# Letting the adding scatters of one expert's blocks be in flight together in a routed feed-forward kernel

## What is computed

```python
x = x + jnp.tanh(g_xattn[0]) * _L0_xattn_ref(_layernorm(x), ctx_512, ...)
x = x + jnp.tanh(g_ffn[0])   * _L0_ffn_ref(_layernorm(x), ...)     # 8 experts, top 2, hidden 192
x = x + jnp.tanh(g_xattn[1]) * _L1_xattn_ref(_layernorm(x), ctx_512, ctx_512, ...)
x = x + jnp.tanh(g_ffn[1])   * _L1_ffn_ref(_layernorm(x), ...)     # 16 experts, top 6, hidden 352
```

```python
weights = jnp.take_along_axis(probs, idx, axis=1)            # idx: the TOP_K experts of a token
cw = jnp.einsum('tk,tke->te', weights, onehot)
h = silu(xf @ W1.T + B1) * (xf @ W3.T + B3)                  # for every expert
y = y + c[:, None] * (h @ W2.T + B2)
```

## Time and profile before

| | |
|---|---|
| median of 3 runs | 2453.0 us (2446.0 to 2457.29) |
| the profiled execution's own time | 2450.1 us |
| its span, first to last instruction | 2448.2 us |
| mean granted TensorE clock | 0.898 of full speed |
| PE busy | 1968.5 us (80%) |
| DVE / ACT / POOL busy | 1245.5 / 815.7 / 1015.5 us |
| HBM traffic | 147 GB/s over the span |
| queue q0 (POOL's DMAs) | 33600 packets, 79.73 MB |

### The profile page before, as it was taken

One profiled execution on the slowest core, in us unless ns is written; L12 is line 12 of the kernel. 1 busy time (PEld: TensorE's weight loads), 2 busy tenths in 40 slices (PEclk: granted clock), 3 DMA queues, 4 the chain that ended last, 5 costly groups with the idle time before them and its releaser, 6 DMA issues. The chain is left out here.

```text
span 2448.2 us, 36252 instructions
## 1 busy us (share of the span) xinstructions
PE 1968.5 (80%) x10825; PEld 1599.1 (65%) x10825; DVE 1245.5 (51%) x2625; ACT 815.7 (33%) x1315; POOL 1015.5 (41%) x795
## 2 busy tenths in 40 slices
PE   4559989886782655878776887899999879999995
PEld 2247767765561443555444676779999778989995
DVE  7864553322221866788875566544444323434442
ACT  3451111132331454565674311113333222323331
POOL 5443644633343566675772110014342333433331
PEclk7779989998895677988988998999999889999998
DMA  8565846977756465221454000094649788474444
GB/s 296 167 241 181 257 126 227 288 229 224 178 116 145 120 152 159 40 36 34 110 149 153 21 29 26 1 338 85 156 80 286 227 280 239 84 224 80 80 80 107
DMA packets 130433, 370.56 MB, mean 151 GB/s; under 512 B 20456, under 2 KB 24424, under 8 KB 125080
## 3 DMA queue, kind: packets, MB, share of 16 engines
q1 hardware_dynamic: 83320, 264.33, 34.2%
q0 software_dynamic: 33600, 79.73, 17.5%
q10 hardware_dynamic: 13344, 24.32, 2.7%
HBM read 209.93 MB, written 149.74 MB: 147 GB/s over the span
## 5 line engine op out<-in xcount | busy, mean ns | idle before, releaser
L1582 PE MATMUL ps<-f_wb,f_xThi 128*128 x2088 | 541.7, 341 | 34.3 <-issue 24.6
L1698 POOL DMA_INDIRECT y_scratch<-f_yo,f_rows x150 | 238.2, 1588 | 495.1 <-ACT f_yo L1426 270.0
L1582 PEld LDWEIGHTS ps<-f_wb,f_xThi 128*128 128x128 f32 x2088 | 375.2, 194 | 63.1 <-issue 53.8
L1582 PE MATMUL ps<-f_wb,f_xTlo 128*128 x1044 | 348.7, 334 | 0.0
L1601 PE MATMUL ps<-f_wb,f_hThi 128*128 (+2 forms) x822 | 281.0, 423 | 16.1 <-DVE f_hTlo L1909 15.6
L728 POOL TENSOR_TENSOR a_elo<-a_e,a_ehi 128x768 f16<-128x768 f32 x128 | 217.4, 1704 | 159.4 <-ACT a_ehi L785 158.0
L1677 POOL DMA_INDIRECT f_xg<-xn_scratch,f_rows x150 | 159.2, 1061 | 217.8 <-PE ps L1566 161.5
L1927 DVE TENSOR_TENSOR f_g<-ps,f_bb 128x352 f32<-128x352 f32 x111 | 58.2, 524 | 342.2 <-PE ps L1582 263.7
L1426 ACT ACTIVATE f_yo<-ps,f_share 128x512 f32<-128x512 f32 x150 | 103.3, 689 | 299.1 <-PE ps L1601 186.4
L1582 PEld LDWEIGHTS ps<-f_wb,f_xTlo 128*128 128x128 f32 x1044 | 202.1, 194 | 0.0
L962 DVE TENSOR_REDUCE a_nmax<-ps 128x1 f32<-128x512 f32 x256 | 163.8, 679 | 48.7 <-PE ps L817 48.3
(11 more groups left out here) (241 smaller groups left out, 3897.6 us busy)
## 6 DMA issues: line engine op xcount, KB each, us to landing
f_wb<-w_scratch SPq DMA_DIRECT2D x16, 2816.0 KB
w_scratch<-f_stage_up SPq DMA_DIRECT2D x27, 1024.0 KB, 5.3
w_scratch<-a_stage_up SPq DMA_DIRECT2D x25, 1024.0 KB, 5.3
f_stage_raw<-in_f_w_dram SPq DMA_DIRECT2D x29, 768.0 KB, 7.4
f_wb<-w_scratch SPq DMA_DIRECT2D x16, 1024.0 KB
w_scratch<-f_stage_down SPq DMA_DIRECT2D x108, 128.0 KB
w_scratch<-a_stage_down SPq DMA_DIRECT2D x100, 128.0 KB, 2.3
f_wb<-w_scratch SPq DMA_DIRECT2D x8, 1536.0 KB
```

The costliest lines, as they stand in the source:

```text
L1582: mm = pe.matmul(out, xt[:, b % 2, k, :], weights(at, w, k, low), start=(m == 0), stop=(m == 3 * KD - 1))
L1698: pool.indirect_dma_start(y_d, bass.IndirectOffsetOnAxis(ap=rows_of[:, b:b + 1], axis=0), yo[:, b % 3, :], None, bounds_check=ROWS + P - 1 ...
```

## The change

Scatters of blocks that belong to the same expert touch different rows (a token is at most once in an expert), so they need not wait for each other. The change counts scatters in three semaphores, `scattered[b % 3]`. A scatter now waits for those of b-1 and b-2, each to a count read from two new rows of `table`: the full count where block b is the first of another expert than b-1, and one scatter less (which has landed anyway) where b and b-1 have the same expert. These counts are made by DVE in `tables`. Only the first blocks of layer 0 have fixed, full counts. The spare rows are tripled, one set for each `b % 3`, so that blocks in flight together don't share a spare row either. ACT's and SP's waits keep their meaning.

```diff
+SPARE = 3 * P
...
-        xn_d = [nc.dram_tensor(f"xn{i}_scratch", (ROWS + P, D + m["E"]), F32, kind="Internal").ap()
+        xn_d = [nc.dram_tensor(f"xn{i}_scratch", (ROWS + SPARE, D + m["E"]), F32, kind="Internal").ap()
...
-        scattered = ctx.enter_context(nc.semaphore("scattered"))
+        scattered = [ctx.enter_context(nc.semaphore(f"scattered{i}")) for i in range(3)]
...
-                    sp.dma_start(g["xn_d"][i][ROWS:ROWS + P, :], zero[:, 0:D + m["E"]]).then_inc(zero_out, 16)
-                    sp.dma_start(g["y_d"][i][ROWS:ROWS + P, :], zero[:, 0:D]).then_inc(zero_out, 16)
+                    for to, width in ((g["xn_d"][i], D + m["E"]), (g["y_d"][i], D)):
+                        sp.dma_start(to[ROWS:ROWS + SPARE, :].rearrange("(r p) d -> p r d", p=P),
+                                     zero[:, 0:width].rearrange("p (o d) -> p o d", o=1).to_broadcast([P, 3, width])
+                                     ).then_inc(zero_out, 16)
...
+        def sums_of(b):
+
+            return 16 * ((EARLIER + 2 - b % 3) // 3 + b // 3 + 1)
+
         def added(eng, b):
 
-            if b > 0:
-                eng.wait_ge(scattered, 16 * (EARLIER + b))
+            if b >= 0:
+                eng.wait_ge(scattered[b % 3], sums_of(b))
...
-                added(sp, BLOCKS)
+                for b in range(BLOCKS - 3, BLOCKS):
+                    added(sp, b)
...
-                    added(act, b - 2)
+                    added(act, b - 3)
...
                     pool.wait_ge(yo_ready, b + 1)
-                    added(pool, b)
+                    past = range(max(b - 2, 0), b)
+                    need = [sums_of(other) if EARLIER + other < 3 else
+                            pool.value_load(table[0:1, 1 + b - other, b:b + 1], min_val=16, max_val=sums_of(other))
+                            for other in past]
+                    for other, value in zip(past, need):
+                        pool.wait_ge(scattered[other % 3], value)
+                        pool.sem_inc(earlier_added, 1)
                     pool.indirect_dma_start(y_d, bass.IndirectOffsetOnAxis(ap=rows_of[:, b:b + 1], axis=0),
-                                            yo[:, b % 3, :], None, bounds_check=ROWS + P - 1,
-                                            compute_op=ALU.add).then_inc(scattered, 16)
+                                            yo[:, b % 3, :], None, bounds_check=ROWS + SPARE - 1,
+                                            compute_op=ALU.add).then_inc(scattered[b % 3], 16)
...
+                    link(dve.tensor_tensor(alike[0:1, 1:BLOCKS], ebf[0:1, 1:BLOCKS], ebf[0:1, 0:BLOCKS - 1],
+                                           ALU.is_equal))
+                    for back in range(1, 3):
+                        for r in range(3):
+                            last = dve.scalar_tensor_tensor(
+                                out=wants[0:1, back - 1, back + r:BLOCKS:3],
+                                in0=iota[0:1, 0:len(range(back + r, BLOCKS, 3))],
+                                scalar=float((EARLIER + 2 - r) // 3 + 1), in1=alike[0:1, back + r:BLOCKS:3],
+                                op0=ALU.add, op1=ALU.subtract)
+                    link(last)
+                    for back in range(1, 3):
+                        dve.tensor_scalar(table[0:1, 1 + back, back:BLOCKS], wants[0:1, back - 1, back:BLOCKS], 16.0,
+                                          None, ALU.mult)
...
-                    link(dve.tensor_scalar(red[:, 0:1], lane[:, 0:1], float(PAD_ROW + 1), None, ALU.add))
-                    link(dve.tensor_scalar(padv[:], at, 0.0, red[:, 0:1], ALU.is_equal, ALU.mult))
+                    for r in range(3):
+                        dve.tensor_scalar(red[:, r:r + 1], lane[:, 0:1], float(PAD_ROW + P * r + 1), None, ALU.add)
+                    link(dve.tensor_copy(padv[:, 0:1], lane[:, 0:1]))
+                    for r in range(3):
+                        last = dve.tensor_scalar(padv[:, r:BLOCKS:3], ps[:, XB, r:BLOCKS:3], 0.0, red[:, r:r + 1],
+                                                 ALU.is_equal, ALU.mult)
+                    link(last)
```

More of the change, by code:

```diff
@@ L80, in build @@
         ps = ctx.enter_context(nc.psum_tensor("ps", [P, 8, 512], F32))
-        xn_d = [nc.dram_tensor(f"xn{i}_scratch", (ROWS + P, D + m["E"]), F32, kind="Internal").ap()
+        xn_d = [nc.dram_tensor(f"xn{i}_scratch", (ROWS + SPARE, D + m["E"]), F32, kind="Internal").ap()
                 for i, m in enumerate(MOE)]
-        y_d = [nc.dram_tensor(f"y{i}_scratch", (ROWS + P, D), F32, kind="Internal").ap() for i in range(2)]
+        y_d = [nc.dram_tensor(f"y{i}_scratch", (ROWS + SPARE, D), F32, kind="Internal").ap() for i in range(2)]
         bias_d = nc.dram_tensor("bias_scratch", (MOE[1]["E"], 2, MOE[1]["H"]), F32, kind="Internal").ap()
@@ L1091, in mixture @@
         share = sb(ctx, tag + "share", [P, BLOCKS])
-        table = sb(ctx, tag + "table", [1, 3, BLOCKS], I32)
+        table = sb(ctx, tag + "table", [1, 5 if BIASED else 4, BLOCKS], I32)
         first_of = sb(ctx, tag + "first_of", [1, E + 1], I32)
@@ L1135, in mixture @@
                 padv = sb(route, tag + "padv", [P, BLOCKS])
+                alike = sb(route, tag + "alike", [1, BLOCKS])
+                wants = sb(route, tag + "wants", [1, 2, BLOCKS])
             room = sb(early, tag + "room", [P, SIZE])
@@ L1191, in mixture @@
         out_done = sem("out_done")
+        earlier_added = sem("earlier_added")
         PARAMS = 16 * (3 if BIASED else 2)
@@ L1678, in gather @@
                                             bass.IndirectOffsetOnAxis(ap=rows_of[:, b:b + 1], axis=0),
-                                            bounds_check=ROWS + P - 1).then_inc(gathered[b % 3], 16)
+                                            bounds_check=ROWS + SPARE - 1).then_inc(gathered[b % 3], 16)
                 pool.wait_ge(up_mm, LAST_U)
@@ L1815, in tables @@
                     e, third, at, need, third_of = (
-                        tnum[0:1, 0, :], tnum[0:1, 1, :], table[0:1, 0, :], table[0:1, 1, :], table[0:1, 2, :])
+                        tnum[0:1, 0, :], tnum[0:1, 1, :], table[0:1, 0, :], table[0:1, 1, :],
+                        table[0:1, 4, :] if BIASED else tnum[0:1, 1, :])
                     link(dve.tensor_copy(e, ebf[0:1, :]))
@@ L1923, in _ @@
                     if BIASED:
-                        buf = dve.value_load(table[0:1, 2, b:b + 1], min_val=0, max_val=2)
+                        buf = dve.value_load(table[0:1, 4, b:b + 1], min_val=0, max_val=2)
                         dve.wait_ge(g_mm, b + 1)
```

## The result

| | before | changed |
|---|---|---|
| median of the runs | 2455.1 us (4 runs, 2446.0 to 2457.3) | 2415.7 us (4 runs, 2406.7 to 2418.2) |
| ratio, 95% interval | 1 | 0.984 (0.9804 to 0.9876) |
| profiled execution | 2450.1, span 2448.2 | 2406.7, span 2404.9 |
| the same kernel once more, beside other runs | 2451.9 | 2408.0, ratio 0.9835 (0.9793 to 0.9877), span of its profile 2393.3 |

The forecast was 2402 us (2384 to 2440). The change took 39 us off, 44 in the second measurement, where 50 to 53 were forecast: faster, as said, by some 80 to 90% of the amount.

A forecast was written before the change was run, and what follows sets the result against it. Layer 0 was taken as bound by the serial scatter chain and fetch-delayed landings, layer 1 by PE. -30 - 9 - 12 - 1.5 + 3 = -49.5 us from 2450.1 gave 2400.6; with the median 2.9 above, forecast 2402 us (2384 to 2440).

The forecast's parts named there:

- The bound: Layer 0: serial scatter chain at 5.70 us a block, 5 us more per weight fetch; layer 1: PE at 6.77.
- POOL's own round is ... 4.7 us (bounds 3.7 and 5.9): POOL's time per block, two table loads at 1.0 us included; under PE's 5.52 and 6.77, so hidden.
- Of the 39.6 us I take three quarters, 30 us: Layer 0, blocks 7 to 38: PE's 39.6 us over its own pace, of which 30 us were to be gained.
- End of layer 0, -9: Last scaling to reload of x: last scatter lands at 757.3 against 766.50 us, 9 us gained (bounds 5 and 10).
- Layer 1, -12: Small experts with back-to-back fetches: 12 of 15.4 us lost over six blocks gained; nothing where PE runs at 6.77.
- End of layer 1, -1.5: After the last scaling: last scatter could start at 2426.3 instead of 2428.34 us; 1.5 us gain taken.
- DVE, +3: Nine small instructions more in `tables`, three in `rows`: 1.0 and 0.5 us, in both layers 3 us, not hidden.
- everything else at nothing: POOL's loads taken as hidden behind PE's pace; zeroing three spare-row sets at the start costs nothing, up to 14 us uncovered.
- The sum: Whole kernel: -30 - 9 - 12 - 1.5 + 3 = -49.5 us; forecast 2402 us, chance 0.68.
- The first rival: Gathers queue behind scatters on POOL's one queue, PE still waits for rows: -23.5 us, about 2428; chance 0.17.
- The second: Long waits all lie at expert changes, only both layers' ends gain: -6 us, about 2447; chance 0.10.
- The third: Dear register loads make POOL's round the bound, 7.0 us at 1.65 each: +29 us, about 2479; chance 0.05.

The follow-up runs named there:

- the runs with one layer alone: Changed kernel with the overlap in layer 0 alone: 2426.8 us, 0.9909 of the kernel before; in layer 1 alone: 2445.9 us, 0.9964.
- the cheap table and POOL's loads first: Changed kernel with constant table parts written earlier, fewer DVE operations on PE's path, and POOL's loads ahead of its wait: 2400.4 us, 0.9791 of the kernel before.
- again: Second profile of the changed kernel, nothing altered, from its repeat beside other runs: 2408.0 us, 0.9835 of the kernel before.

## Why the prediction was right, and where it wasn't

- **The bound.** Right. Layer 0 was set by the chain of scatters at 5.70 us a block and by its slow landings beside fetches. Two experiments bear it out: a faster PE alone changes nothing, and the overlap with all else equal is worth 34 us there.
- **"POOL's own round is ... 4.7 us (bounds 3.7 and 5.9)".** Too long. It is 3.26: I added the loads to a round in which they are hidden, and added 0.75 us for the next start where 0.30 is enough once the scatter has nothing to wait for. The lower bound that the text gave for the loads, nothing, was the right end, for a POOL that is behind. Beside it, the Trainium skill, page "DMA: Bandwidth & Descriptors", section on latency and other measured facts, has a floor of about 0.6 us for a register load. The measured median on POOL is 0.289 us; the measurement decides, and the page's price would have been too high.
- **"Of the 39.6 us I take three quarters, 30 us".** About right. Over the six profiles with this loop the blocks of layer 0 gained 21.5, 32.1, 28.9, 28.3, 26.8 and 23.5 us, 27 in the mean.
- **End of layer 0, -9.** -8.3 and -8.8, right. With POOL's loads ahead of the wait it is -10.1, -10.1 and -10.2.
- **Layer 1, -12.** Too small: -17.9. I let the small experts keep a fifth of their loss because they "still drain at each change". They do (11.7 us at one scatter), but POOL catches up 3.5 us with each block, not the 2.1 that a round of 4.7 gives, so that nothing reaches PE. This is the same error in POOL's round, seen from the other side; with the round lengthened to 5.06 the gain went.
- **End of layer 1, -1.5.** Wrong, +0.4 and +0.8. The last scatter starts 4.57 us after the scaling, as before (4.52). Before, the result was there at 2424.51 us and the landing that POOL waited for at 2426.28, 1.8 us later. In the changed kernel this wait is gone, but the two loads with their register work and the waits behind them take the same 1.8 us there (2380.78 to 2382.60, one load of them 0.86). With the loads ahead of the wait the 1.3 us come. And the forecast took 0.75 us from the counts to the start, where the last scatter of layer 1 needs 2.06 in the kernel before, in the changed one (2382.60 to 2384.66) and with the loads first; what these 2.06 us are isn't known.
- **DVE, +3, and everything else at nothing.** This is the step that failed. The additions cost 12 us (7 to 18). DVE's own part was nearly right: PE's waits for its sums, at tables and rows of layer 0 and of layer 1, grew from 2.50, 0.76, 2.13 and 0.97 us before to 3.85, 1.20, 3.49 and 1.42 in the run with full counts, 3.6 us together. What was put at nothing without a reason is what longer waits do to PE's clock, 1.3 to 1.8 us in layer 1 wherever it stayed at half speed for 6.8 us, and the loads where nothing hides them, 1.5 us over the two ends with full counts. These come to 6.4 to 6.9 us, the low end of what was measured. The rest is not placed.
- **The sum.** That the gains came out at 52 us for 52.5 is in part luck. By the runs with one layer alone layer 0 gave 34 us, where 39 were forecast with its end, and layer 1 gave 21, where 13.5 were: two errors that cancel. And the forecast's own sum is off by 1.5 us: -49.5 from 2450.1 and 2.9 more for the median make 2403.5, not 2402.
- **A cost not thought of: PE's own loads.** The prediction priced PE's table loads as bounds for POOL's and never asked what POOL does to PE's. In the changed kernel's profile the second of them took about 0.3 us in 24 of the 39 passes of layer 0 and 0.7 to 1.5 in nine. Two of them, the first beside a gather (698.03 to 699.09), the second beside a scatter:

```profile
L1625 PEldq TENSOR_LOAD <-f_table x1: 969/969/969, 698.3 to 698.3; - x1
...
L1625 PEldq TENSOR_LOAD <-f_table x1: 300/300/300, 612.6 to 612.6; - x1
```

- **The first rival (gathers become the bound), 0.17.** Did not come about: the 27.9 us are gone. Part of it stays possible: PE waited 7.9 us for gathered rows with its loads apart, 6.8 with POOL's loads tripled and 3.7 with the cheap table and POOL's loads first. The Trainium skill, page "DMA: Bandwidth & Descriptors", section on queues, rings and completion order, has each DMA engine switch between queues packet by packet; by that rule, read as in the prediction, gathers would be stuck behind scatters. No wait of PE shows it in the changed kernel. The runs with such waits don't tell a queue full of scatters from the traffic of the fetch, beside which the late gathers were issued.
- **The second (hardly any effect), 0.10.** Excluded by 52 us between full and relaxed counts.
- **The third (POOL slower), 0.05.** Far off: a round of 3.26. But its point was set too high. I had put it at a round of 6.77; the tripled loads show that a round of 5.06 already costs 17 us.

Open: attention 1 has the same code in all these kernels, and from the reload to the first step of mixture 1 the profiles of the thirteen others lie between 3.5 us under and 12.8 over that of before; the granted clock over that stretch was 0.80 to 0.82 in them and 0.82 before. What sets it isn't known. It may hold part of the 12 us.

## What to carry to other kernels

Price a sequencer's instruction by where it stands: behind an engine that is behind its work it is free, in front of an awaited result it is paid whole, so loads go ahead of the wait. When a serial chain is loosened, ask how fast the follower catches up between two forced stops, not only whether its mean round is under the pace. And small instructions on an engine that PE already waits for are paid whole, and the longer wait can cost once more by keeping PE's clock down; before a longer wait is put down to them, compare the work ahead of them in the two traces.

## What the runs showed of the hardware

- A load of a table value into a register takes 0.3 us, but up to 1.5 us at times. In layer 0 of the changed kernel 14 of PE's second loads began while POOL made the descriptors of a gather, with a median of 0.475 us, and 6 while it made those of a scatter, with 0.302; in "again" 7 with 0.381 and 10 with 0.298. The longest, 1.54 us, began beside neither, so this is a tendency and not a cause that is shown.
- Two loads in a row on PE's sequencer cost PE time: apart, its pass falls from 5.52 to 5.36 us.
- Behind a wait of 2.1 to 4.8 us in the shared part PE was granted half of its speed, in the kernel before as in the others, in some profiles for 3.4 us and in others for 6.8.
- A small operation of DVE that takes 0.17 us took 0.46 to 0.65 beside a cast of POOL, in layer 0's tables of all fourteen profiles.
- Scatters started 3.26 us apart hardly slow each other. In the run with the cheap table and POOL's loads first the four started from 573.67 to 583.46 us took 4.9 to 5.2 us from start to landing, for the 4.95 of a single one before; each overlapped the next by less than 2 us. The slow ones beside a fetch took 9 to 12 us.
